# First attention of a fused two-layer kernel: scores in pairs of PSUM banks, maxima in single banks turned by VectorE, whole sums two steps behind, and unread matmuls ahead of and between the first maxima

## The reference, cut to what matters

```python
xn = _layernorm(x, axis=-1)                  # x: (8, 512, 128)
q = split_heads(_binlinear(x, Wq, bq))       # H = 16 heads, Dh = 8
k = split_heads(_binlinear(x, Wk, bk))
v = split_heads(_binlinear(x, Wv, bv))
att = jnp.einsum('bhtd,bhsd->bhts', q, k) * scale
att = jax.nn.softmax(att, axis=-1)
y = jnp.einsum('bhts,bhsd->bhtd', att, v)
y = y.transpose(0, 2, 1, 3).reshape(B, T, C)
return _binlinear(y, Wp, bp)
```

## Time and profile before

| | us |
|---|---|
| median of 3 runs (lowest, highest) | 990.36 (990.01, 994.16) |
| profiled execution, its own time | 992.35 |
| span of that execution in the profile | 990.5 |

### The profile page before, as it was taken

The page is one execution under the profiler, slowest core; times in us unless marked ns, Lnnn a source line. Parts: engine busy times, 40 slices in busy tenths (PEclk is TensorE's granted clock), DMA queues, the critical chain, the costliest instruction groups (busy, mean ns, idle before and its releaser), DMA issues. The chain is left out here.

```text
span 990.5 us, 18391 instructions
## 1 busy us (share of the span) xinstructions
PE 897.2 (91%) x6674; PEld 461.9 (47%) x6674; DVE 695.5 (70%) x1054; ACT 634.7 (64%) x1383; POOL 366.1 (37%) x355
## 2 busy tenths in 40 slices
PE   4699999999999999979998989899769999999997
PEld 2333444344434344448888878332223444444443
DVE  7879888898989999613333338878867767766654
ACT  4468677778777878852322222476557778777875
POOL 4013030214343333005556542255645547554300
PEclk9579899999999999989999989999789999999999
DMA  7615525140414000036766553259977999999800
GB/s 226 250 39 207 230 71 211 40 162 27 176 45 151 28 26 25 8 98 181 209 198 199 164 176 96 54 111 136 144 88 75 108 110 101 103 104 112 92 12 22
DMA packets 80973, 114.30 MB, mean 115 GB/s; under 512 B 12946, under 2 KB 58004, under 8 KB 78452
## 3 DMA queue, kind: packets, MB, share of 16 engines
q1 hardware_dynamic: 73684, 94.87, 48.2%
q0 software_dynamic: 6352, 17.86, 5.3%
q10 hardware_dynamic: 848, 0.40, 0.1%
HBM read 56.00 MB, written 33.57 MB: 90 GB/s over the span
## 5 line engine op out<-in xcount | busy, mean ns | idle before, releaser
L989 DVE TENSOR_REDUCE a_nmax<-quad 128x2 f32<-128x1024 f32 x256 | 302.1, 1220 | 32.4 <-PE quad L603 29.9
L798 ACT ACTIVATE a_probs<-bank 128x512 f32<-128x512 f32 x339 | 190.8, 598 | 53.0 <-PE bank L620 36.9
L1873 ACT ACTIVATE a_late<-quad 128x256 f32<-128x256 f32 (+3 forms) x512 | 180.4, 461 | 37.3 <-PE quad L1642 36.6
L2028 DVE SCALAR_TENSOR_TENSOR a_late<-a_late,const 128x512 f32<-128x512 f32 x128 | 117.8, 928 | 73.8 <-ACT a_late L1873 73.5
L632 PE MATMUL av<-a_probs,a_va 128*32 128x256 f32 x2048 | 166.1, 397 | 0.9 <-ACT a_probs L798 0.6
L603 PE MATMUL quad<-k_stack,q_stack 24*128 24x512 f32 x512 | 133.6, 523 | 9.9 <-DVE a_nmax L989 5.8
L620 PE MATMUL bank<-q_stack,k_stack 26*128 26x512 f32 x339 | 136.8, 504 | 2.8 <-DMA q_stack<-a_nparts 2.0
L798 ACT ACTIVATE a_probs<-misc 128x512 f32<-128x512 f32 x173 | 103.4, 598 | 28.9 <-PE bank L620 16.2
L1642 PE MATMUL quad<-q_stack,k_stack 96*128 96x256 bf16 (+3 forms) x512 | 104.1, 305 | 7.4 <-ACT a_late L1873 3.7
L1653 PE MATMUL av<-a_late,a_va 128*32 128x512 f32 (+3 forms) x1024 | 96.1, 448 | 8.1 <-DVE a_late L2039 7.1
L508 POOL DMA_INDIRECT sorted_rows<-x_rows,a_slot x64 | 62.4, 974 | 107.5 <-PE av L632 105.0
(11 more groups left out here) (304 smaller groups left out, 1406.1 us busy)
## 6 DMA issues: line engine op xcount, KB each, us to landing
spread<-a_parts SPq DMA_DIRECT2D x48, 256.0 KB
q_stack<-a_parts SPq DMA_DIRECT2D x96, 128.0 KB, 7.4
k_stack<-a_parts SPq DMA_DIRECT2D x96, 128.0 KB, 7.8
wu<-packed_weights SPq DMA_DIRECT2D x20, 384.0 KB
m_wu<-packed_weights SPq DMA_DIRECT2D x19, 384.0 KB
q_stack<-spread SPq DMA_DIRECT2D x7, 1024.0 KB
k_stack<-spread SPq DMA_DIRECT2D x7, 1024.0 KB
sorted_rows<-in_shape_constants POOLq DMA_DIRECT2D x5, 1040.0 KB, 5.4
```

What stands on the lines that cost most here:

```text
L798: act.activation(probs[:, (GH * s + j) % 8, :], col_bank(n)[:, :], ACT.Exp, scale=scale).then_inc(col_free, 1)
L989: dve.tensor_reduce(nmax[quad % 2][:, at:at + 2 * TT:TT], row_slot(n)[:, :, :], AX_X, ALU.max, negate=True)\
L1873: act.activation(probs[:, (64 * b + n) % 12, kt * P:T], quad[:, n % 4, kt * P:T], ACT.Square, bias=1.0, scale=0.25)\
L2028: dve.scalar_tensor_tensor(out=blocks, in0=blocks, scalar=1.0, in1=S["tri"][:, None, :].broadcast_to([P, GH, P]), op0=ALU.add, op1=ALU.mul ...
```

## The change

- **Banks.** `units` and `unit_no` replace rows and columns. Scores go into `quad`, two heads at a time into one of two pairs of banks (`scores`, L639 in the new file). Each pair is read by one exponential of 128x1024 (L820). The maxima go into the three single banks, one head each (`maximum`, L626), and VectorE reduces 128x512 to 128x1 (L1043), four times a step.
- **Order in a step.** Maximum, two scores, maximum, whole sums, maximum, two scores, maximum, extras. All extras share the two pairs with the scores.
- **Maxima to rows.** VectorE turns blocks of 32 by 32 (`dve.transpose`, L1048, into `ntop`). PE's turn and the split are gone. One row instead of two is subtracted (25 rows in a score), and SyncE sends four DMAs instead of eight. Maxima are six steps ahead (`AHEAD = 6`), and the turn of quad q stands behind the first maximum of step 4q + 4, so in step 4q - 2.
- **Whole sums** are of step s - 2 (`LAG = 2`), in one half of 512 columns, with 12 buffers of `probs`.
- **Readers.** ScalarE reads what was gathered, projected, the logits and the counts (`read_gathered`, `read_projected`, `read_logits`, `read_counts`). VectorE inverts 128x32 from SBUF, POOL multiplies (`scale_rows`) and adds the bias (`add_bias`). In the last batch VectorE reads PSUM as before.
- **Unread matmuls.** `idle(4, T)` puts four matmuls of 512 columns ahead of the first maxima, and `idle(1, P)` one of 128 columns behind each of the first 24. They write `av`, which nobody reads until the first whole sums start it anew.
- **Places.** All extras stand one step later in their batch, the routing one step too. Its scratch lies in `S["wu"]`, so the loads of unit weights wait for step 42 of the routing instead of 32. `yT` is `full[0]`, so `read_y` waits for POOL's split of q.

```diff
-        AHEAD = 8
+        AHEAD = 6
-        ROWS = 16 * 2 * GH
+        ROWS = 16 * GH
-        GATHER_AT, TURN_AT, PROJECT_AT, QK_AT, VALUES_AT = (1, 3), 5, 7, (9, 11), 13
+        GATHER_AT, TURN_AT, PROJECT_AT, QK_AT, VALUES_AT = (2, 4), 6, 8, (10, 12), 14
-        ROUTE_AT = 4
+        ROUTE_AT = 5
+        LAG = 2
...
+        def pair_of(n):
+            return S["quad"][:, 2 * ((n - SINGLES) % 2):2 * ((n - SINGLES) % 2) + 2, :]
...
             def max_rows(quad):
                 b, c = quad // NG, quad % NG
-                wait(sp, row_free, row_no["turn", quad, 0] + 1)
-                for i in range(2 if quad else 1):
-                    for j in range(GH):
-                        row = STRIP * j + HROWS + i
-                        sp.dma_start(qs[b % 4][row:row + 1, c, :], nparts[TT * j:TT * (j + 1), i, :].bitcast(F32))\
-                          .then_inc(rows_in[quad % 2], 16)
+                wait(sp, turned, quad + 1)
+                rows = qs[b % 4][HROWS:HROWS + STRIP * (GH - 1) + 1:STRIP, c, :].rearrange("r (t q f) -> r t q f", t=TT, q=P // STRIP)
+                for q in range(P // STRIP):
+                    sp.dma_start(rows[:, :, q, :], ntop[quad % 2][STRIP * q:STRIP * q + TT * GH, :]).then_inc(rows_in[quad % 2], 16)
...
+            def scale_rows(b, u):
+                wait(pool, rec, 2 * b + u + 1)
...
+            def group(s, i):
+                if s + AHEAD < LAST:
+                    maximum(s + AHEAD, 2 * i)
+                scores(s, i)
+                if s + AHEAD < LAST:
+                    maximum(s + AHEAD, 2 * i + 1)
...
+                r = (k + 2) % GH
+                at = slice(STRIP * r, STRIP * r + HROWS)
+                wait(pe, max_free, n - 2)
+                pe.matmul(max_banks[n % 3][:, :], qs[b % 4][at, c, qt * P:(qt + 1) * P].bitcast(F32R),
+                          ks[b % 4][at, c, :].bitcast(F32R), start=True, stop=True).then_inc(max_mm, 1)
...
+            idle(4, T)
             for s in range(-AHEAD, 0):
-                maxima(s + AHEAD, 0)
-                if s + AHEAD == TT:
-                    turn(0)
-                maxima(s + AHEAD, 1)
+                for k in range(GH):
+                    maximum(s + AHEAD, k)
+                    idle(1, P)
...
             for s in range(LAST):
                 b, t = s // 16, s % 16
-                score(s, 0)
-                score(s, 1)
-                if s + AHEAD < LAST:
-                    maxima(s + AHEAD, 0)
-                if s >= 1:
-                    weigh(s - 1, 0)
-                score(s, 2)
-                score(s, 3)
-                if s + AHEAD < LAST:
-                    maxima(s + AHEAD, 1)
+                group(s, 0)
+                if s >= LAG:
+                    weigh(s - LAG)
+                group(s, 1)
...
-                if s >= 1:
-                    weigh(s - 1, 1)
-                if (s + AHEAD) % TT == 0 and s + AHEAD <= LAST:
-                    turn((s + AHEAD) // TT - 1)
...
-            def exps(s):
-                for j in range(GH):
-                    n = col_no["s", s, j]
-                    if j == 0:
-                        wait(act, av_mm, s - 1)
-                    wait(act, col_mm, n + 1)
-                    act.activation(probs[:, (GH * s + j) % 8, :], col_bank(n)[:, :], ACT.Exp, scale=scale).then_inc(col_free, 1)
+            def exps(s, i):
+                n = unit_no["s", s, i]
+                if i == 0:
+                    wait(act, av_mm, s - PROBS // GH + 1)
+                wait(act, unit_mm, n + 1)
+                at = (GH * s + 2 * i) % PROBS
+                act.activation(probs[:, at:at + 2, :], pair_of(n), ACT.Exp, scale=scale).then_inc(unit_read, 1)
...
+            def maximum(m, k):
+                n, quad, qt = GH * m + k, m // TT, m % TT
+                at = TT * ((k + 2) % GH) + qt
+                wait(dve, max_mm, n + 1)
+                dve.tensor_reduce(nmax[quad % 2][:, at:at + 1], max_banks[n % 3][:, :], AX_X, ALU.max, negate=True).then_inc(max_free, 1)
+
+            def turn(quad):
+                wait(dve, max_free, GH * TT * (quad + 1))
+                wait(dve, rows_in[quad % 2], ROWS * (quad // 2))
+                dve.transpose(ntop[quad % 2][:, :], nmax[quad % 2][:, :]).then_inc(turned, 1)
```

505 lines of the change are left out of this document (259 added, 246 removed).

## The result

The changed kernel takes 1011.4 us (median of four runs, 1010.9 to 1022.4) against 990.2 before on the same chip: ratio 1.025, 95% interval 1.019 to 1.031. In a second set of runs, on another chip, it was 1.035 (1.030 to 1.040). So it is 2.5 to 3.5% slower, where 985.0 us was forecast, and outside the range of 972 to 1003. Ratios with an interval leave out executions over 1.5% above the fastest of their kernel; medians take all.

What follows compares the result with a forecast made beforehand. VectorE's reductions of maxima were taken as the bound, starved by PE's extras. Main stretch -6.3, front +0.2, tail -0.6, with 1.3 kept back, gave -5.4 on the median of 990.36: 985.0 us, range 972 to 1003.

Steps and rivals of the forecast that it cites:

- Ring of 2.70 us: Each first-stage step: second maximum, whole sums, third maximum, its reduction, then the next second maximum; 2.70 us a step.
- Extras: Gather, projection and the like in steps 3 to 119: 47 extras delay the scores, 0.34 us each.
- Stretch of steps without falls and late rows: Steps 3 to 119: 117 x 2.70 + 47 x 0.34 = 331.9 us, plus 1.0 for turns, reciprocals and routing.
- Late rows: Steps 16, 20 and 40: scores wait for rows of maxima behind POOL's transfers, 3 x 1.4 = 4.2 us.
- the clock: Main stretch: PE's granted clock falls behind three late rows, one and a half falls at 2.7 us, 4.0 us.
- Rival (b): Steps: 0.4 us of idle PE in each makes the clock fall outside late rows, 2.7 us a fall; chance 0.12.
- The front: Before step 3: unread matmuls raise the clock, first score five us later, steps 0 to 2 faster; 0.2 us lost.
- Rival (d): Front: the clock stays at 0.50 throughout, step 3 some 18 us later, 1003 us in all; chance 0.08.
- The tail: Step 120 to the last sum: 19.4 us against 20.0 before, 0.6 less.
- Sum: Whole kernel: -6.3 (main stretch) + 0.2 (front) - 0.6 (tail) = -6.7 us, cut to -5.4.
- The 1.3 us that the forecast kept back: Reserve held from the forecast gain for steps in which ring and extras add up: 1.3 us.

Runs made afterwards that it cites:

- no_unread_again: The changed kernel without any unread matmul, run a second time beside the changed kernel: ratio to before 1.014 (1.010 to 1.019).
- slow_reduce_full: `half_no_unread` with one more VectorE reduction of 512 columns in each step, its result unread: ratio to before 1.054 (1.049 to 1.059).
- half: The changed kernel with whole sums again in two halves of 256 columns, unread matmuls kept: median 1011.7 us against 990.2 before.
- half_no_unread: The changed kernel with whole sums in two halves of 256 columns and no unread matmul: ratio to before 0.995 (0.992 to 0.998).
- no_unread: The changed kernel without any unread matmul, neither the four of 512 columns nor the 24 of 128: ratio to before 1.017 (1.010 to 1.024).

## Why the prediction was wrong, point by point

- **Ring of 2.70 us: right.** 2.70 was measured, by the terms of the sum. Reductions of 512 columns last 0.68 and come 0.61 apart, as taken, and a turn takes 0.20 us (0.25 taken). The Trainium skill's 120 cycles a read of PSUM ("VectorE: DVE Perf Modes", The TRN2 errata), an estimate of 2.63 us for four (0.66 each), fits the length of a single one, but not the pace of queued ones: in halves a step of 2.38 us holds four.
- **Extras: nearly right.** A pair of steps, one with an extra, took 5.69 (turn of y), 5.84 (projection) and 5.90 us (first gather), so 0.3 to 0.5 above 2 x 2.70, where 0.34 was taken. The exponential of 1024 columns took 1.023 against 1.02 (the two terms written for it add up to 1.03). A late batch without q and k took 45.0 us (355.7 to 400.7 in `no_unread_again`), against 44.9 by the forecast's terms. It took 45.0 before too, so there was no gain to be had in the late batches.
- **Stretch of steps without falls and late rows:** 356.2 - 15.5 - 5.5 = 335.2, against 331.9 + 1.0 forecast. Right within 1%.
- **Late rows: right in mechanism and nearly in size,** 5.5 us against 4.2, at steps 16, 20 and 40 as forecast (2.40, 0.86 and 2.26, where 1.4 each was taken).
- **The step that failed: the clock.** It was put at one and a half falls, 4.0 us. There were five in the steps, 44.3 us, 15.5 us lost (61 us in the second profile). Rival (b) named the mechanism (0.4 us idle in every step; the trace shows 0.34 to 0.40 at one place, 0.87 in all) and was given 0.12, "against it: the matmuls per step are the same and the steps shorter". That is the flaw: it counted matmuls, not the time in which PE streams. That fell from 1.98 of 2.24 us in a plain step to 1.83 of 2.70. `slow_reduce_full` shows the same by VectorE alone: 1.98 of 2.99, and 145 us at the lower clock where halves have 85.
- **The front: sign and size failed.** +0.2 was forecast; +8.6 to +20 came (step 3 at 73.0, 80.5 and, in `half`, 84.7). Of it 24 x (0.84 - 0.70) = 3.4 us is the pair of maximum and unread matmul at the full clock: the unread one takes 0.42 (36.02 to 36.44), where 0.28 was taken from matmuls of one kind in a row. The rest is that the clock fell again. Its rise came as forecast (the four unread ones ended at 35.6, against 36.6), but the forecast assumed that it then stays. Rival (d), given 0.08, had the clock low all through the front and step 3 some 18 us later; what came lies between the two.
- **The tail:** +3.9 against -0.6, by a fall at 439.9 us and the late rows of step 124. There steps hold no maxima and are shorter, and the rows' lead of a fixed number of steps shrinks with them (argued, not tested).
- **Sum.** Falls in steps +11.5 over forecast, front +8.4, tail +4.5, late rows and rest of the steps +3.6: 28, less 2.5 in stages that the change leaves alone. That is 25.5, and -6.7 + 25.5 = +18.8, against a measured 18.6. The 1.3 us that the forecast kept back lie inside the rest of the steps. These are the shares of one profile; in the second the front alone took 16.

## What to carry to other kernels

Before a matmul is moved between a producer and its reader, work out the ring through that reader, and then how much of the new step PE streams, not how many matmuls it holds. Here steps with 0.87 of 2.70 us idle lost 4 and 6% to the lower clock in two profiles, and steps with 0.40 of 2.38 under 1% in two. Unread matmuls gained nothing in a front that VectorE bounds, and cost 2% where they kept small matmuls from running beside one another. Where falls move from one execution to the next, compare the clock over all runs before reading a cause out of one profile.

## What the runs showed of the hardware that was not expected

- The granted clock fell to 0.50 (at 265.8 us) in steps in which PE's longest idle time was 0.4 us. It also fell behind a stretch in which matmuls of 24 rows and of 128 rows stood without a gap (at 54.2 us; modelled busy time 20.50 of the 20.50 us before it).
- Two executions of one program have their falls at different places, for 17.0 and for 34.1 us at the front. The times scatter with them: the four runs of `half` spread over 22 us, the ten of `half_no_unread` over 19.
- At the lower clock the loop can stay there long: 34.1 us in batch 0 of `no_unread`, in steps of 4.16 and 6.30 us.
- The same kernel before took 976.6, 990.2, 990.2 and 994.1 us on four chips.
